# A differential attention kernel: second projections in four pairs, a double buffer in the attention's tail, and sums moved between pairs

## The reference, cut to what matters

```python
q1 = heads(x @ Q1_w.T); k1 = heads(x @ K1_w.T + K1_b)
q2 = heads(x @ Q2_w.T); k2 = heads(x @ K2_w.T + K2_b)
v = heads(x @ V_w.T)
a1 = softmax(einsum('bhqd,bhkd->bhqk', q1, k1) / scale)
a2 = softmax(einsum('bhqd,bhkd->bhqk', q2, k2) / scale)
o = einsum('bhqk,bhkd->bhqd', a1 - lam * a2, v)
y = groupnorm(o) @ out_w.T + out_b
```

## Time and profile before

| | us |
|---|---|
| median of 3 runs | 6351.29 |
| lowest, highest | 6344.42, 6355.15 |
| the profiled execution | 6343.51 |
| its span | 6341.7 |

### The profile page before, as it was taken

How to read it: one execution, slowest core, us unless ns; L and a number is a source line. 1 busy time by engine, 2 the same in 40 slices (tenths; PEclk the granted TensorE clock), 3 DMA queues, 4 the chain that set the end, 5 groups by cost and what they waited for, 6 DMA issues and landing times.

```text
span 6341.7 us, 127068 instructions
## 1 busy us (share of the span) xinstructions
PE 5935.0 (94%) x41264; PEld 3784.5 (60%) x41264; DVE 4638.3 (73%) x6519; ACT 3218.9 (51%) x5724; POOL 3091.0 (49%) x1382
## 2 busy tenths in 40 slices
PE   6999999999999999999999999999999999999999
PEld 4565565655656556565565756656565565655656
DVE  5767777677776777767777677777777767677776
ACT  4545545455554545535455354554545545455454
POOL 3716537175370744707447073471735617256272
PEclk9999999999999999999999999999999999999999
...
GB/s 74 56 49 54 58 51 51 59 49 56 53 46 59 54 55 50 46 58 55 54 52 45 62 54 53 51 48 57 55 51 53 47 60 56 46 57 44 65 56 44
DMA packets 148338, 339.05 MB, mean 53 GB/s; under 512 B 38224, under 2 KB 60880, under 8 KB 139216
## 3 DMA queue, kind: packets, MB, share of 16 engines
...
...
## 4 chain that ended last, share of the span: by engine, by line
PE 70%; DVE 14%; issue 7%; ACT 4%; DMA 3%; SPq 1%; DVEq 0%; ACTq 0%
PE psum L997 16%; PE psum L1214 13%; PE psum L1145 12%; PE psum L1166 11%; DVE minus_max L742 6%; PE psum L1273 6%; PE psum L1173 4%; DVE recip_sum L763 2%; PE psum L1242 2%; DVE stage L737 2%; DMA stack<-stage 2%; PE psum L1193 1%; PE psum L1046 1%; ACT probs L497 1%; PE psum L1151 1%
## 5 line engine op out<-in xcount | busy, mean ns | idle before, releaser
L354 POOL TENSOR_TENSOR prob_sums<-probs 128x1024 f32<-128x1024 f32 x752 | 1794.4, 2386 | 3055.0 <-ACT probs L497 2629.8
L497 ACT ACTIVATE probs<-psum 128x512 f32<-128x512 f32 x4096 | 2222.6, 595 | 1428.0 <-PE psum L1214 1417.6
L742 DVE TENSOR_REDUCE minus_max<-psum 128x1 f32<-128x1024 f32 x2048 | 2417.6, 1207 | 415.7 <-PE psum L1145 410.8
L1214 PE MATMUL psum<-stack 98*128 98x512 f32 x4096 | 1451.3, 432 | 43.4 <-ACT probs L497 43.4
L1145 PE MATMUL psum<-stack 96*128 96x512 f32 x4096 | 1261.0, 414 | 129.8 <-DVE stage L737 70.7
L354 POOL TENSOR_TENSOR prob_sums<-prob_sums,probs 128x1024 f32<-128x1024 f32 x512 | 1220.2, 2383 | 72.1 <-ACT probs L497 35.7
L1166 PE MATMUL psum<-probs,v_tokens 128*32 128x256 f32 x16384 | 1111.8, 388 | 0.0
L1214 PEld LDWEIGHTS psum<-stack 98*128 98x128 f32 x4096 | 713.6, 191 | 581.0 <-ACT probs L497 447.4
L1145 PEld LDWEIGHTS psum<-stack 96*128 96x128 f32 x4096 | 725.3, 192 | 472.7 <-DVE minus_max L742 129.1
L997 PE MATMUL psum<-act_hi,w_hi 128*128 128x512 f32 x1730 | 702.3, 406 | 45.3 <-issue 26.7
L1166 PEld LDWEIGHTS psum<-probs,v_tokens 128*32 128x32 f32 x16384 | 429.0, 109 | 474.6 <-issue 297.9
...
## 6 DMA issues: line engine op xcount, KB each, us to landing
stack<-stage SPq DMA_DIRECT2D x1024, 128.0 KB, 3.1
stack<-stage SPq DMA_DIRECT2D x256, 256.0 KB, 3.0
prob_sums<-combine_rows_dram SPq DMA_DIRECT2D x128, 256.0 KB, 3.8
stage<-combine_rows_dram SPq DMA_DIRECT2D x128, 256.0 KB, 4.1
...
x_tile<-o_head SPq DMA_DIRECT2D x512, 32.0 KB, 1.9
stack<-max_rows SPq DMA_DIRECT2D x512, 4.0 KB
...
```

Source lines behind the costliest of these rows:

```text
L354: nc.gpsimd.tensor_tensor(total, first, probs[:, k % NP, :], ALU.add).then_inc(sum_pool, 1)
L497: nc.scalar.activation(probs[:, k % NP, half * HALF:(half + 1) * HALF], ps[:, 4 + half, :], ACT.Exp).then_inc(p_ready, 1)
L742: v.tensor_reduce(nm[:, u % 2, q:q + 1], flat_in, AX.X, ALU.max, negate=True).then_inc(ring_free, 1)
L1214: mm(ps[:, 4 + half, :], stack[0:KS, s, 1, kt * P:(kt + 1) * P], stack[0:KS, s, 0, half * HALF:(half + 1) * HALF], start=True, stop=True). ...
```

## The change

- **Second projections.** Four pairs, (5, 1) to (6, 0), take one whole projection each. On TensorE its two halves stand one behind the other between the first and the second score of the pair, ahead of the odd tile's transposed scores; ScalarE copies both ahead of the odd tile's exponents.
- **Start of an image.** The fourth projection is split into two parts that stand behind the second and the third score of unit 0. Three of the eight value tiles move ahead of the first score, the others stand behind scores 0 and 3 to 6. ScalarE and VectorE take the 1024-column projections in halves. SP issues the loads of stacks 0 and 1 in finer steps, the high parts as soon as ScalarE has written them, and loads stack 2 ahead of stack 1.
- **Sums.** Both late group sums (groups 1 and 2 of the unit before) stand in pair 0. The first half of the reciprocals stands ahead of the maximum of tile 2, the second stays at tile 5, head_out moves to tile 7, the statistics to tile 1 of the next even unit.
- **Tail.** From the tile at (14, 4) on, odd tiles use banks 2 and 3 for their transposed scores, so that these need not wait for the exponents of the even tile. The small matmul of the group norm uses banks 0 and 4.
- **Output projection.** Its high-part matmuls wait for the high parts alone, eight of them stand ahead of the second small matmul; one VectorE step for the low part moves behind another.

VectorE's stream at the start of an image, before: all four projections, then maxima.

The diff, cut to its core:

```diff
-    late = {2: (u, 0), 0: (u - 1, 1), 1: (u - 1, 2)}.get(pair)
-    return [late] if late and late[0] >= 0 else []
+    late = {2: ((u, 0),), 0: ((u - 1, 1), (u - 1, 2))}.get(pair, ())
+    return [(v, g) for v, g in late if v >= 0]
...
-PROJ_BESIDE = ((5, 1), (5, 2), (5, 3), (6, 0), (6, 1), (6, 2), (6, 3), (7, 0))
+PROJ_BESIDE = ((5, 1), (5, 2), (5, 3), (6, 0))
...
-    before = [("proj", t) for t in range(4)] + [("score", 0, q) for q in range(NT)] + [("turn", 0)]
+    before = [("proj", 0), ("proj", 1), ("proj", 2), ("score", 0, 0), ("score", 0, 1), ("part", 3, 0, 0), ("score", 0, 2),
+              ("part", 3, 1, 0)]
+    before += [("score", 0, q) for q in range(3, NT)] + [("turn", 0)]
     before += [("score", *divmod(n, NT)) for n in range(NT, AHEAD)]
...
-            beside[u, pair] = []
-            for kt in (2 * pair, 2 * pair + 1):
-                n = u * NT + kt + AHEAD
-                if n < UNITS * NT:
-                    beside[u, pair].append(("score", *divmod(n, NT)))
+            items = [("score", *divmod(n, NT)) for n in (u * NT + 2 * pair + AHEAD, u * NT + 2 * pair + 1 + AHEAD)
+                     if n < UNITS * NT]
+            if (u, pair) in PROJ_BESIDE:
+                items[1:1] = [("part", PROJ_BESIDE.index((u, pair)), half, 1) for half in range(NH)]
             if pair == TURN_AT and u + 1 < UNITS:
-                beside[u, pair].append(("turn", u + 1))
-            if (u, pair) in PROJ_BESIDE:
-                beside[u, pair].append(("part", *divmod(PROJ_BESIDE.index((u, pair)), 2)))
+                items.append(("turn", u + 1))
+            beside[u, pair] = items
...
+VALUES_BEHIND = {("proj", 2): (0, 1, 2), ("score", 0, 0): (3,), ("score", 0, 3): (4,), ("score", 0, 4): (5,),
+                 ("score", 0, 5): (6,), ("score", 0, 6): (7,)}
...
+TAIL = UNITS * NT - AHEAD
+LAST_EVEN = (len(RING) - 1) // 2 * 2
+def exp_bank(k):
+    return 2 if k >= TAIL and k % 2 else 4
...
-RECIP_AT, HEAD_AT = (4, 5), 6
+RECIP_AT, HEAD_AT = (2, 5), 7
...
+                    if u < 2:
+                        last = [RING_AT["proj", t] if ("proj", t) in RING_AT else RING_AT["part", t, 1, 0] for t in range(4)]
+                        sp.wait_ge(proj_hi, b * PROJ_STEPS + 4 * m + 2)
+                        sp.dma_start(*q_parts[1]).then_inc(stack_in[s], 16)
+                        sp.wait_ge(ring_free, b * len(RING) + last[2 * m] + 1)
+                        sp.dma_start(*q_parts[0]).then_inc(stack_in[s], 16)
+                        sp.wait_ge(proj_hi, b * PROJ_STEPS + 4 * m + 4)
+                        for dst, src in k_parts[:2]:
+                            sp.dma_start(dst, src).then_inc(stack_in[s], 16)
+                        sp.wait_ge(ring_free, b * len(RING) + last[2 * m + 1] + 1)
+                        sp.dma_start(*k_parts[2]).then_inc(stack_in[s], 16)
+                        return
...
-                for u in range(NST):
+                for u in (0, 2, 1):
                     load_stack(u)
...
+                def project(t):
+                    act.wait_ge(ring_full, b * len(RING) + RING_AT["proj", t] + 1)
+                    for half in range(NH):
+                        take_projection(t, half, 0, wide(RING_AT["proj", t] % 2)[:, half, :])
+                def project_part(t, half, g):
+                    act.wait_ge(ring_full, b * len(RING) + RING_AT["part", t, half, g] + 1)
+                    take_projection(t, half, g, wide(RING_AT["part", t, half, g] % 2)[:, 0, :])
+                for t in range(3):
+                    project(t)
+                copy_values(0)
+                copy_values(1)
+                act.wait_ge(y_out[1], b * 16 + 16)
+                for half in range(NH):
+                    project_part(3, half, 0)
+                copy_values(2)
+                copy_values(3)
...
-                        for item in BESIDE.get(divmod(k // 2 - 1, PAIRS), []) if kt % 2 == 0 else []:
+                        for item in BESIDE[u, kt // 2] if kt % 2 else []:
...
-                        t, cols = item[1], slice(0, N)
-                        if item[0] == "part":
-                            cols = slice(item[2] * HALF, (item[2] + 1) * HALF)
-                            flat_in = wide(n % 2)[:, 0, :]
-                        dve.wait_ge(proj_hi, b * PROJ_STEPS + (4 + 2 * t + item[2] if item[0] == "part" else t) + 1)
+                        t = item[1]
+                        pieces = [(half, half, 0) for half in range(NH)] if item[0] == "proj" else [(item[2], 0, item[3])]
+                        for half, at, g in pieces:
+                            cols = slice(half * HALF, (half + 1) * HALF)
+                            dve.wait_ge(proj_hi, b * PROJ_STEPS + 8 * g + 2 * t + half + 1)
...
                     dve.wait_ge(g_full, b * CT + t + 1)
-                    groups = ps[:, 2 + 2 * t, 0:4].rearrange("p (a s) -> p a s", s=2)
...
+                def ahead_of_score(u, kt):
+                    if u and kt == RECIP_AT[0]:
+                        sum_recips(u - 1, 0)
                 def beside_score(u, kt):
-                    if u and kt in RECIP_AT:
-                        sum_recips(u - 1, RECIP_AT.index(kt))
+                    if u % 2 == 0 and u >= 4 and kt == 1:
+                        head_statistics((u - 4) // 2)
+                    if u and kt == RECIP_AT[1]:
+                        sum_recips(u - 1, 1)
                     if u and kt == HEAD_AT:
                         head_out(u - 1)
-                    if u % 2 and u >= 3 and kt == NT - 1:
-                        head_statistics((u - 3) // 2)
+                    if u == UNITS - 1 and kt == NT - 1:
+                        head_statistics(HEADS - 2)
...
-                norm_low(0, 1)
                 for half in range(NH):
                     cols = slice(half * HALF, (half + 1) * HALF)
+                    if half == 0:
+                        norm_low(0, 1)
...
-                    if item[0] == "score" and item[1] == 0:
-                        values(item[2])
+                    for tt in VALUES_BEHIND.get(item, ()):
+                        values(tt)
...
-                                if k >= 1:
+                                if k == TAIL + 1:
+                                    pe.wait_ge(ring_free, b * len(RING) + LAST_EVEN + 1)
+                                elif k > TAIL:
+                                    pe.wait_ge(p_ready, b * 2 * UNITS * NT + 2 * k + half - 3)
+                                elif k >= 1:
                                     pe.wait_ge(p_ready, b * 2 * UNITS * NT + 2 * k + half - 1)
-                                mm(ps[:, 4 + half, :], stack[0:KS, s, 1, kt * P:(kt + 1) * P],
+                                mm(ps[:, exp_bank(k) + half, :], stack[0:KS, s, 1, kt * P:(kt + 1) * P],
                                    stack[0:KS, s, 0, half * HALF:(half + 1) * HALF], start=True,
                                    stop=True).then_inc(st_full, 1)
-                            if kt % 2 == 0:
-                                for item in BESIDE[u, pair]:
-                                    if item[0] == "score":
-                                        ring_step(item)
+                            behind = 3 if (u, pair) in PROJ_BESIDE else 2
+                            for item in BESIDE[u, pair][slice(0, behind) if kt % 2 == 0 else slice(behind, None)]:
+                                if item[0] != "turn":
+                                    ring_step(item)
...
-                            if item[0] != "score":
+                            if item[0] == "turn":
...
+                def project_out(kt, half, low):
+                    pe.wait_ge(on_lo if low else on_hi, b * NH * CT + NH * kt + half + 1)
+                    cols = slice(half * HALF, (half + 1) * HALF)
+                    for k in (2 * half, 2 * half + 1):
+                        w = W_O + kt * C + (k % 2) * P
+                        for n, (wt, xx) in enumerate(((wh, xl),) if low else ((wh, xh), (wl, xh))):
+                            last = mm(ps[:, k, :], wt[:, w:w + P], xx[:, kt, cols],
+                                      start=(kt == 0 and not low and n == 0), stop=(kt == CT - 1 and low))
+                        if kt == CT - 1 and low:
+                            last.then_inc(y1_full, 1)
+                for half in range(NH):
+                    project_out(0, half, False)
                 norm_groups(1)
-                for kt in range(CT):
-                    for k in range(4):
-                        half = k // 2
-                        pe.wait_ge(on_lo, b * NH * CT + NH * kt + half + 1)
-                        for n, (wt, xx) in enumerate(((wh, xh), (wl, xh), (wh, xl))):
-                            w = W_O + kt * C + (k % 2) * P
-                            last = mm(ps[:, k, :], wt[:, w:w + P], xx[:, kt, half * HALF:(half + 1) * HALF],
-                                      start=(kt == 0 and n == 0), stop=(kt == CT - 1 and n == 2))
```

(7 more changed lines are left out.)

59 lines of the change are left out of this document (23 added, 36 removed).

## The result

| | kernel before | changed kernel |
|---|---|---|
| median of 17 runs each, us | 6343.57 | 6328.11 |
| lowest, highest | 6331.62, 6355.15 | 6318.13, 6337.48 |
| span of the profiled execution | 6341.7 | 6324.6 |

The ratio is 0.9976 (95% interval 0.997 to 0.9983). The change makes the kernel faster by 15 us, a third of the 48 us of the forecast. The span became 17.1 us shorter, 1.07 us an image. The question is where the other 1.9 us an image went.

A forecast was written before the change was run, and what follows sets the result against it. TensorE, busy for 94% of the span, was taken as the bound. Terms of -5.7 + 2.1 + 2.8 - 2.2 = -3.0 us an image, times 16, gave 6351.3 - 48 = 6303 us; range 6258 to 6360, chance 0.8.

The forecast's parts named there:

- second projections: Units 5 to 7: four changed pairs cost 12.0 us over plain ones against 17.65, -5.7 us an image.
- moved sums: Units 1 to 14: a sum added to pair 0, part returned as a vanished wait, +2.1 us an image.
- start of the image: First score 1.1 us earlier, two parts among the maxima cost 3.9, +2.8 us an image.
- tail: last exponents: Attention's end: GpSimd's adds run on at once, last exponents end 2.0 us earlier an image.
- tail: output projection: Eight matmuls come earlier and win 0.2 of VectorE's 0.66 us wait for the last matmuls.
- the 6.4 of the prediction: Units 5 to 7: bound of the second projections term without any wait, -6.4 us an image.
- a unit becomes 0.43 - 0.28 = 0.15 longer, 14 times: Units 1 to 14: sum adds 0.43 us to pair 0, 0.28 of wait comes back, +2.1 an image.
- -1.0, where TensorE is at half clock: Tail: weaker end of the -2.2 us term, for TensorE at half clock in the output projection.
- The slow clock spreads: Rival: clock falls at the image's start and unit 0's slow stretch lengthens, +1.4 us an image, 6374; chance 0.12.
- a low clock before the first transposed scores: Image start: one of the signs named as showing the forecast wrong; no size given.
- The moved sums cost in full: Rival: each of 14 units 0.55 us longer, term 7.7 instead of 2.1, 6393 us; chance 0.06.
- The waits only move: Rival: part pairs keep a wait of 0.65 us each, -0.3 us an image, 6346; chance 0.12.

The follow-up runs named there:

- e3: Changed kernel with sums, reciprocals, head output and statistics put back where they were before the change: 6285.78 us, ratio to the kernel before 0.9908.
- e5: Changed kernel with the tail's double buffer undone, all transposed scores in banks 4 and 5 again: 6364.43 us, ratio to the kernel before 1.0032.
- e1: Changed kernel with the output projection of before, all 24 matmuls behind the second small matmul: 6322.93 us, ratio to the kernel before 0.9964.
- e2: Changed kernel with the second small matmul ahead of the eight early high-part matmuls: 6319.33 us, ratio to the kernel before 0.9959.
- e9: Changed kernel plus matmuls nobody reads, filling TensorE's waits around unit 0 and in the output projection: 6266.45 us, ratio to the kernel before 0.9879.
- e8: Changed kernel with sums, image start and output projection as before, plus unread matmuls in TensorE's waits: 6165.52 us, ratio to the kernel before 0.9715.
- e11: Kernel before plus unread matmuls ahead of the first turn, two scores of unit 1 and the second small matmul: 6296.42 us, ratio 0.9925.
- e6: Changed kernel with the second projections as eight parts in eight pairs again: 6444.1 us, ratio to the kernel before 1.0151.
- e10: Changed kernel with VectorE's reciprocals, head output and statistics as before, both late sums still in pair 0: 6383.24 us, ratio to the kernel before 1.0063.
- e4: Changed kernel with the fourth projection whole ahead of the first score and value tiles behind unit 0's scores: 6291.49 us, ratio to the kernel before 0.991.
- e12: Kernel of e8 with high-part matmuls waiting for high parts alone and the second small matmul first: 6168.32 us, ratio to the kernel before 0.9723.

## Why the prediction was right in its sign and wrong in its size

| term, us an image | forecast | measured | by |
|---|---|---|---|
| second projections | -5.7 | -6.1 | units 5 to 7: before 60.24, e3 54.17 |
| moved sums | +2.1 | +3.2 | changed kernel against e3 |
| start of the image | +2.8 | +2.85 | -1.07 and +3.92 |
| tail: last exponents | -2.0 | -2.20 | e5 gives it back alone |
| tail: output projection | -0.2 | +1.32 | e1, e2, e9 |
| unit 0 | 0 | -0.16 | less than traces differ by (15.5 to 16.5); e8, e9, e11 |
| sum | -3.0 | -1.1 | |

**What bounds the kernel: right.** TensorE is the bound, and each term was read at the right wait.

**Second projections: right.** The four pairs last 6.82, 6.46, 6.04 and 6.89 us against 3.74, 3.53, 3.10 and 3.97 of plain ones, 11.9 more together where 12.0 was forecast. No score waits for a low part. e6 shows the same step from the other side, 6.84 in the surroundings of the moved sums. One bound of this term does not follow from the rows: without any wait the eight parts' own matmuls leave 17.65 - 8 x 1.48 = 5.8, not the 6.4 of the prediction.

**Moved sums: the term mis-sized, 3.2 for 2.1.** The step that failed here is "a unit becomes 0.43 - 0.28 = 0.15 longer, 14 times". The mechanism held in every point: pair 1 stays at 3.74 and is ended by the maxima, the waits in pair 0 vanish, and e10 shows that VectorE's moves remove them. But the wait of one unit was taken for all. Pair 0 without any wait is 3.53, as in unit 1 of before; all of pairs 0 are now 3.97. They were 3.81 to 3.83 in odd units (+0.15), 3.74 to 3.77 in most even ones (+0.22) and 3.54 in unit 1 (+0.43). In (6, 0), which holds a projection, there was no wait to win either: 6.46 in e3 and e8, 6.89 now. Pair (7, 2) takes 3.69 where e3 has 3.54. The row of pair 0 over all units would have shown this before the run.

**Start: right in both halves.** The loads bring the first score 1.07 forward (forecast 1.1), and the two parts cost 3.92 (forecast 3.9), with VectorE idle for 1.30 and 1.35 and at work for 0.75 twice. That the first number agrees to 0.03 is partly luck: all traces with these loads give 0.55 to 1.08. e4 shows that the parts could have been spared, and that without them the finer loads keep only 0.27. That the loads of stack 1 behind stack 2 cost nothing was not tested by itself.

**Last exponents: right.** -2.20 for -2.0, with GpSimd's adds in a row as the prediction said.

**Output projection: the step that failed.** The prediction counted eight matmuls that come earlier, as a gain of 0.2 at no price, and bounded the clock's effect by "-1.0, where TensorE is at half clock". It missed three things.

First, the early matmuls are in front of the small matmul in TensorE's queue. At the low clock they hold it up until 745.45, and VectorE, with the whole second half of the group norm, waits 0.79 for it. About 0.5 of the stretch is this, by the estimate at e2; the rest of the 0.79 would be a wait for a DMA.

Second, eight matmuls taken out of a block of 24 leave an idle time of 2.18 in it, and the clock falls at the start of the second block again: from 749.76 its matmuls start 0.43 us apart, against 0.23 at the full clock. In e1, with the old order, the low clock lasts as long, but a third of it falls on idle time, and the block has its second half at the full clock. e2 takes the first and the second away together and wins 1.15.

Third, the moved low part stands behind a step that waits for a DMA as soon as the small matmul is in time (e12).

With the clock at 1.00 everywhere the new order takes 14.95 (e9) and the old one 14.55 (e11), and e12 puts its own part of the order at 0.45. So by these differences 0.4 of the 1.32 is the order at the full clock, for which e12's rows show the wait for the moved low part, and 0.9 comes with the low clock, in the small matmul's way and in the second block. In the changed kernel's shorter tail the old order takes 15.40 (e1), 0.22 less than in the kernel before, so against e1 the new order costs 1.54.

The Trainium skill (TensorE: Matmul & The Clock Gate, section "HAM oscillation — how this bites in real kernels") says that work in pieces shorter than the waits between them can keep finding the clock low. The output projection agrees only in part: the clock falls for each of its two blocks, but the waits ahead of them (2.07 and 2.18 us) are shorter than the work between them (4.6 us, 742.16 to 746.72), and each block still begins at 1.00 in the image shown. What the Trainium skill says in the section "A second HAM failure mode: psum-queue depth-cycling" of the same page, on frequent short idle times, and which the prediction weighed for the start, is borne out only in part as well. Units 5 to 7 of the changed kernel have short waits (0.61 ahead of a turn at 582.00) and a clock of 1.00 in all images. With eight parts in these units the clock fell there in two of 16 images of e6 and of e11, which made them 1.6 and 2.7 us longer. Ahead of unit 0 the clock falls (0.60 from 493 to 497), and with those waits filled it does not.

**The rivals.** "The slow clock spreads" did not happen where it was put: the clock is 1.00 through the two parts of the start, and unit 0 is no longer than before. The prediction's sign of being wrong, a low clock before the first transposed scores, did come, in 15 of 16 images. It could not tell much, for the kernel before shows it in 11 of 16, and it cost little: filled, this stretch is 0.40 shorter in e9 and 0.27 in e11. The low clock did spread in the output projection, where the prediction had looked only for a smaller gain. "The moved sums cost in full" (7.7) was refuted as such, though a fifth of the difference to it came true. "The waits only move" gave nearly the measured time (6346 against 6328, from a median of 6351 that later runs put at 6344) for a reason that did not occur. The range held the time, by its width: the centre was 1.9 us an image too low, 1.5 of it in the output projection, 1.1 in the sums, less 0.7 of small gains elsewhere. Of the forecast gain of 3.0 us an image, 1.1 was left.
